# Graph network with four residual LayerNorm layers: the products of the third and fourth residual kept in PSUM

## The reference

```python
x = layernorm(x + L0(x, adj))   # (adj @ (x W + b)) / row sums of adj
x = layernorm(x + L1(x, adj))   # relu((adj @ x) W), masked
x = layernorm(x + L2(x, adj))   # relu(An @ x @ W + bias), An = D^-1/2 (adj + I) D^-1/2
x = layernorm(x + L3(x, adj))   # H = x W0 + T(x W1) + T(T(x W2)) + biases, relu(H)
                                # T = rows of adj * exp(leaky_relu(attention)), divided by their sums
```

## Time and profile before

| | |
|---|---|
| time of the kernel, median of 3 runs | 631.95 us (630.64 to 632.51) |
| span of the profiled execution | 628.7 us |
| median less that span | 3.25 us |
| VectorE busy | 584.5 us, 93% of the span |
| TensorE busy | 549.4 us, 87% |
| GpSimd busy | 484.5 us, 77% |
| ScalarE busy | 424.1 us, 67% |
| DMA | mean 71 GB/s |

### The profile page before, as it was taken

How to read it: one execution, slowest core, us unless ns; L and a number is a source line. 1 busy time by engine, 2 the same in 40 slices (tenths; PEclk the granted TensorE clock), 3 DMA queues, 4 the chain that set the end, 5 groups by cost and what they waited for, 6 DMA issues and landing times.

```text
span 628.7 us, 12633 instructions
## 1 busy us (share of the span) xinstructions
PE 549.4 (87%) x4044; PEld 513.7 (82%) x4044; DVE 584.5 (93%) x1597; ACT 424.1 (67%) x937; POOL 484.5 (77%) x575
## 2 busy tenths in 40 slices
PE   5678998988989889989999889898999899986982
PEld 5578888987879878988889878798789898886872
DVE  3779999999999999999999999999999999999766
ACT  5367786587865868578774778658775677755653
POOL 3787889787887889878897878878898787874243
PEclk9979999999999999999999999999999999999997
DMA  8524002330032300322023301223003300101001
GB/s 286 208 67 119 18 18 83 103 111 24 33 100 67 133 17 17 111 89 100 17 60 108 115 33 33 100 67 133 17 17 100 100 35 2 52 18 67 1 1 67
DMA packets 25223, 44.73 MB, mean 71 GB/s; under 512 B 3184, under 2 KB 3824, under 8 KB 25200
## 3 DMA queue, kind: packets, MB, share of 16 engines
q1 hardware_dynamic: 24336, 43.79, 21.4%
q10 hardware_dynamic: 864, 0.66, 0.4%
HBM read 36.05 MB, written 8.39 MB: 71 GB/s over the span
## 4 chain that ended last, share of the span: by engine, by line
DVE 61%; PE 18%; issue 9%; POOL 4%; ACT 3%; SPq 2%; DMA 2%; DVEq 0%; ACTq 0%; POOLq 0%
DVE stats L975 10%; DVE nod_lo L1020 5%; DVE X L1033 4%; PE pair L259 4%; DVE X L1067 4%; DVE fea_lo L966 4%; DVE P L1061 4%; DVE P L1054 4%; PE pair L261 3%; PE pair L260 3%; DVE nod_lo L1015 3%; DVE powin L987 3%; DVE tmp L1041 3%; DVE mv L982 3%; PE ring L259 2%
## 5 line engine op out<-in xcount | busy, mean ns | idle before, releaser
L766 POOL TENSOR_TENSOR rstd<-powin,minus_half 128x2 f32<-128x2 f32 (+1 forms) x128 | 106.7, 834 | 76.4 <-DVE nmean L988 76.4
L565 ACT ACTIVATE X<-X,nmr,rstd 128x256 f32<-128x256 f32 x192 | 103.6, 592 | 44.8 <-POOL nmr L775 44.8
L975 DVE BATCH_NORM_STATS2 stats<-X 128x6 f32<-128x256 f32 x256 | 94.1, 410 | 1.6 <-POOL X L759 1.2
L259 PE MATMUL ring<-adj_hi,nod_lo 128*128 128x256 f32 x256 | 76.0, 297 | 19.8 <-DVE nod_lo L1020 13.4
L259 PE MATMUL ring<-W_hi,fea_lo 128*128 128x256 f32 x256 | 72.7, 284 | 1.4 <-DVE fea_lo L966 1.4
L260 PE MATMUL ring<-adj_lo,nod_hi 128*128 128x256 f32 x256 | 73.2, 286 | 0.0
L261 PE MATMUL ring<-adj_hi,nod_hi 128*128 128x256 f32 x256 | 73.2, 286 | 0.0
L261 PE MATMUL ring<-W_hi,fea_hi 128*128 128x256 f32 x256 | 71.8, 281 | 0.0
L260 PE MATMUL ring<-W_lo,fea_hi 128*128 128x256 f32 x256 | 71.6, 280 | 0.0
L259 PEld LDWEIGHTS ring<-adj_hi,nod_lo 128*128 128x128 f32 x256 | 49.6, 194 | 24.6 <-DVE nod_lo L1020 15.7
L966 DVE TENSOR_TENSOR fea_lo<-ring,fea_hi 128x512 fp32r<-128x512 f32 x96 | 63.3, 679 | 3.6 <-ACT fea_hi L486 3.5
(11 more groups left out here) (110 smaller groups left out, 2206.0 us busy)
## 6 DMA issues: line engine op xcount, KB each, us to landing
adj_in<-adjT_dram SPq DMA_DIRECT2D x64, 256.0 KB, 3.0
xT_in<-xT_dram SPq DMA_DIRECT2D x32, 256.0 KB, 3.7
X<-x_dram SPq DMA_DIRECT2D x32, 256.0 KB, 2.7
out_dram<-X SPq DMA_DIRECT2D x32, 256.0 KB, 2.0
P<-wk_dram SPq DMA_DIRECT2D x3, 256.0 KB, 8.2
P<-w_dram SPq DMA_DIRECT2D x2, 256.0 KB, 7.8
X<-bk_dram SPq DMA_DIRECT2D x3, 128.0 KB, 7.3
P<-w_dram ACTq DMA_DIRECT2D x1, 256.0 KB, 4.1
```

The source lines that it names most:

```text
L259: mm(o, lhs(1, t, i), rhs(0, t), start=t == 0, stop=False)
L565: last = nc.scalar.activation(nodes(X[min(l + 1, 3)][g])[:, t, :], nodes(X[l][g])[:, t, :], ACT.Identity, scale=rstd[l][g][:, t:t + 1], bi ...
L766: tt(rstd[l][g][:, 0:n], powin[l][g][:, 0:n], minus_half[:, 0:n], ALU.pow).then_inc(rstd_ready[l], 1)
L975: last = nc.vector.bn_stats(stats[l][g][:, 6 * t:6 * t + 6], nodes(X[l][g])[:, t, :])
```

## The change

The scaled product of both residuals is written back into `ring[g]`, over the product that it was computed from, and the residual op reads it there. The residual op of the fourth layer takes the plain 512-column form. As `ring[g]` is now read until `y3` is done, `s5` waits for `y3` of its slot and not for `z3`. (The line numbers stay: no line is added or removed.)

```diff
                 if not first:
-                    pe.wait_ge(z3_ready, count(g, kn - 1))
+                    pe.wait_ge(y_ready[3][g], kn)
                 product(halves(g), cols(nod, g), rows(adj, g)).then_inc(s5_done[g], 1)
...
                 for t in range(2):
-                    last = stt(tmp[g][:, t * F:(t + 1) * F], ring[g][:, t * N:(t + 1) * N], rstd[0][g][:, 2 + t:3 + t], b2_bc[:, :],
-                               ALU.mult, ALU.add)
+                    half = ring[g][:, t * N:(t + 1) * N]
+                    last = stt(half, half, rstd[0][g][:, 2 + t:3 + t], b2_bc[:, :], ALU.mult, ALU.add)
                 last.then_inc(z2_ready, 1)
...
-                stt(X2[g][:, :], tmp[g][:, :], 0.0, X2[g][:, :], ALU.max, ALU.add).then_inc(y_ready[2][g], 1)
+                stt(X2[g][:, :], ring[g][:, :], 0.0, X2[g][:, :], ALU.max, ALU.add).then_inc(y_ready[2][g], 1)
...
                 for t in range(2):
-                    last = stt(mixed(P0[g])[:, t, 0:F], ring[g][:, t * F:(t + 1) * F], rinv[g][:, t:t + 1], mixed(P0[g])[:, t, 0:F],
-                               ALU.mult, ALU.add)
+                    half = ring[g][:, t * F:(t + 1) * F]
+                    last = stt(half, half, rinv[g][:, t:t + 1], mixed(P0[g])[:, t, 0:F], ALU.mult, ALU.add)
                 last.then_inc(z3_ready, 1)
...
-                stt(nodes(X3[g]), mixed(P0[g])[:, :, 0:F], 0.0, nodes(X3[g]), ALU.max, ALU.add).then_inc(y_ready[3][g], 1)
+                stt(X3[g][:, :], ring[g][:, :], 0.0, X3[g][:, :], ALU.max, ALU.add).then_inc(y_ready[3][g], 1)
```

## The result

The changed kernel takes 607.83 us, the median of four runs (607.37 to 611.09), where the kernel before took 631.3 us beside it (four runs, 630.54 to 632.51). The ratio is 0.963, with a 95% interval of 0.960 to 0.966: 23.5 us less, a little over twice the 11.1 us that were forecast, and outside the range of 612 to 629.5 us. The profiled execution's span fell from 628.7 to 605.7 us. The `stt` of `y2` and of `z3` stands one line lower within its loop, so they are now lines 1028 and 1062; no other line moved.

The account below looks back on a forecast made before the run. It took a closed path to bound the kernel: TensorE's gapless 13.30 us, then VectorE's stretch of 59.66 us. Rounds 10.7, plus end 1.2, minus PSUM writes 0.8, gave 11.1 us less: 620.8 us, range 612 to 629.5 us.

Parts of the forecast that it names:

- The form of `y1` for both ops: On VectorE, `y2b` and `y3` would each take 0.67 us like `y1`, 21.5 us less VectorE time in all.
- The three steps of VectorE's stretch: Savings at `y2b(2)` 0.86, `y2b(3)` with `x1_lo(0)` 0.45 and `y3(1)` 0.96 us: 2.27 us for each iteration.
- The start of `s5(3)`: On TensorE, `s5(3)` would wait for `y3(3)` and start 0.74 us later each time, delaying its 13.3 us stretch.
- The writes to PSUM: Halves of `y2` and `z3` written to PSUM cost 0.01 us more each, 78 on the path: 0.8 us.
- The fixed price of PSUM: Rival: each VectorE write to PSUM costs some 0.06 us, 4.7 us in place of 0.8: 624.7 us, chance 0.14.
- What is removed, in VectorE's stretch, for each iteration: Step placing savings between `sums0(2)` and the next `s5(3)`: 2.27 us for each iteration, ends 1.2 and 2.4.
- lie in TensorE's stretch: nothing: Savings of `y2b(0)` and `y2b(1)` count nothing, since VectorE would only wait longer for `s2(2)`.
- seven rounds: Net gain of 1.53 us a round, with the 0.74 us wait charged each time, taken seven times: 10.7 us.
- the holding-up moves on: Rival: other VectorE operations meet GpSimd's instead; half comes back, 628.6 us, chance 0.15; all, 637.1 us, chance 0.04.
- the whole 21.5 us come through: Rival: all VectorE time saved on `y2b` and `y3` counts, with `s5(3)` starting no later: 610.5 us, chance 0.08.
- My terms at their best: High ends of the terms, 7 x (2.4 - 0.74) + 1.67 + 2.3, gave 15.6 us gained, so 616.4 us.

Follow-up runs that it names:

- e4: The kernel before, with `y2b` taking its second tensor from the product in `ring` (PSUM) in place of residual `X2`: 620.18 us, 0.977 of the kernel before.
- e6: The kernel before, with `y2` writing its product into `ring` while `y2b` still reads `tmp`: 632.79 us against 632.29, 1.000.
- e11: The changed kernel run once more, unaltered, as base for two others on the same chip: 612.16 us, 0.966 of the kernel before.
- e3: The kernel before with one edit, `s5` waiting for `y3` of its slot and not for `z3`: 640.41 us, 1.010 of the kernel before.
- e7: The changed kernel, with GpSimd's bias on the next input cut to four columns: 595.41 us, 0.940 of the kernel before.
- e1: The kernel before with the third residual's change alone (`y2` and `y2b`): 619.48 us, 0.978 of the kernel before.
- e13: The changed kernel with slot 3's fourth residual in its old form, `xT_hi_part(2)` behind `z0(1)` and `variance_eps(1, 1)` behind `statistics(1, 2)`: 600.47 us, 0.952 of the kernel before.

## Why the prediction was wrong

**Right, in mechanism and size.** The form of `y1` for both ops: 677 and 667 ns on average for the 0.67 us taken, none over 0.70. The three steps of VectorE's stretch in the round that was read, 2.27 us forecast and 2.28 measured. The start of `s5(3)`, +0.82 for +0.74, with line 1067 as its releaser. The writes to PSUM, 9 ns a half where I took 10. The Trainium skill, "SBUF — State Buffer", section "Who interferes with whom", lets VectorE and GpSimd shut each other out where VectorE has two SBUF inputs, and also where it runs in a two-port mode, for which the page names `tensor_scalar` among others; the prediction left that second case out of its rule. `e4` agrees with the first: with one of two tensors in PSUM, 674 ns on average. The rows of `nmean`, a `tensor_scalar`, agree with the second (0.15 to 1.33 us). The fixed price of PSUM in "VectorE: DVE Perf Modes", section "The TRN2 errata — SBUF-src ops pay a fixed extra latency per instruction", in the Trainium skill, is one for reads; it shows neither for them (670 against 672 ns) nor for the writes, for which I had tried it: 482 against 473 ns, and the time of `e6`.

**Wrong: what else gets shorter.** The step that failed is "What is removed, in VectorE's stretch, for each iteration", which took three operations of one round for the whole. I had seen there that a GpSimd operation was 1.74 us long and not 1.29 because it "itself stood behind `y2b(3)`", and used it once. A two-tensor operation of VectorE can delay GpSimd elsewhere too; GpSimd's later operations then stand where other VectorE operations want to start, and those are held in turn. GpSimd is busy for 17.7 us less, and VectorE for 5.4 us less in the operations that are not `y2b` or `y3` (26.8 less 21.4): lines 1015 and 1020 have 2.0 us less each, line 988 has 1.1 and line 1006 has 0.6. Of these I had counted `x1_lo(0)` alone. In the round shown, `xd_lo(3)` and `variance_eps(2, 1)` give 0.82 us beside a forecast net of 1.53. `xd_lo(3)` gives its part in all five rounds; the 0.48 us of `variance_eps(2, 1)` are those of this round, and line 987 as a whole stays at 273 ns.

**Wrong: `y2b(0)` and `y2b(1)` "lie in TensorE's stretch: nothing".** In the steady rounds the stretch from `s5(3)` to `sums0(2)` gave 3.44 us of 14.13. Where `y2b(1)` took 1.48 us (the round from 279.66) and where it took 1.38 (from 500.42) VectorE did not wait for `s2(2)`, and the saving counted. In three rounds more, TensorE itself had idle time there, 1.96 us together, which the forecast did not have; the later `s5(3)` took it up, so that "0.74 us later, each time, and with it all 13.3 us" charged the wait too high. Rows 1, one gapless stretch of 13.30 us, had stood for all. In the changed kernel VectorE waits 0.88 us at `y2(0)` and 0.57 at `sums0(2)`, where I had foreseen some 1 us at the second alone.

**Wrong: one round taken for seven.** The round that I read, 72.96 us, was one of the short ones; two of the kernel before were 74.6 and 74.5 us, because `nmean` had met `alpha(3)` in them. But the changed kernel has two such rounds as well, so these meetings explain nothing of the mean gain of 2.83 us against the 2.44 of the one shown; the shorter `s5(3)` to `sums0(2)` does (0.69 us on average against 0.13). As `e11` shows, how many long rounds an execution has differs between executions of one kernel, so some of the difference between two spans need not be the change's doing. The ratios of the three sets of runs, 0.963 to 0.966, hold that in.

**The start** gained 4.25 us for 1.53. The first 0.50 us are there before the first changed instruction (62.15 us for 62.65), so they are not the change's. `y2b(0)` and `y2b(1)` took 1.38 and 1.37 us here, of which 0.65 us arrived at `sums0(2)`, and a meeting of `nmean` was gone (1.18 us), which can fall either way. `xd_lo(3)` gave 0.3 to 0.4 us as in the rounds.

**Wrong: "seven rounds" for the wait.** The row at 568.56 is not the start of `s5(3)`, as I took it, but that of `s5(2)` in the last such iteration, where VectorE is behind and TensorE waits earlier too. There the wait of `s5(3)`, 0.57 us, is not the one on the path, so I charged 0.74 us once too often. From there to the end the gain was 1.75 us for 1.2: `y3(0)` -0.70 and `y3(1)` -0.96 as forecast, `variance_eps` gave back 0.36 us and not 0.47, and close to 0.5 us came from a wait of VectorE in between (0.37 us, behind `y2` at 581 us) that is gone.

**The rivals.** The sign of "the holding-up moves on" was wrong: little came back (the means of lines 1020, 1015 and 987 did not grow), and what moved on was a gain. The total is near "the whole 21.5 us come through", 610.5 us, but not by its way: `s5(3)` did start later. Of what that rival asked for, TensorE freed elsewhere, a part was there all the same, in its idle time ahead of `s2(2)`. That the total came near it is luck. My terms at their best gave 616.4 us, the range went to 612, and the measured time is 4 us below that; the sentence that below 616.4 "lies what I have not seen" was a reason for a wider one.

**Left open.** The 1.6 us of `e3` beyond the wait, if they are real, and why `e7` gained 14 us, are explained only in part by the rows given. That a shorter GpSimd queue makes the untouched VectorE operations shorter is read from the rows and from `e1`, `e4` and `e7`; no run moves one of GpSimd's operations by itself. That `nmean` could be freed in `e13` too was not tried.

## What to carry to other kernels

Where two engines shut each other out, price it for both, and go through every operation of the pair, the small ones wholly in one memory too: what is taken out of the pair shortens the others. Read several rounds before one of them stands for all, and the first and last iterations by themselves; that a stretch of an engine has no gap has to be seen in each. Before a wait is removed, or a new one is charged, follow the other chains that start at the same event. Here a store and the load queued behind it were about as late as the wait: each of the two removed alone gained nothing clear of the noise, both together gained the wait.

## What the runs showed of the hardware that I had not expected

- An operation of 128 x 2 elements on VectorE, wholly in SBUF, takes 0.15 us or 1.33 us where its start and that of a GpSimd operation of 1.29 us are recorded within 0.03 us of each other. The same kernel had spans of 605.7 and 610.5 us.
- The holding is mutual: GpSimd's lines 759 and 754 went from 1434 and 1439 ns to 1322 and 1293 without a change to them, and GpSimd's busy time fell where VectorE lost its second SBUF tensor (`e4`, 476.1 us) and not where VectorE wrote to PSUM (`e6`, 484.1, against 484.5).
- VectorE reads and writes one PSUM bank in place for 9 ns more than a write to SBUF (482 against 473 ns for 256 columns).
- `y2b`, untouched, went from 1063 to 1233 ns when only a semaphore of TensorE changed (`e3`): a start that came 0.81 us later changed which operations meet.
